# The Mamba block between two attention stacks: chunks of 512 tokens, decays and B read from PSUM, one input product on POOL

## What is computed

```
x = x + 0.5 * ffn_stack(layernorm(x))
x = x + mamba(layernorm(x))
x = x + 0.5 * ffn_stack(layernorm(x))

def mamba(x):                                   # D_INNER 256, D_STATE 16, DT_RANK 64
    h = x * rsqrt(mean(x * x) + 1e-5) * norm_w
    u, res = split(h @ in_w, 2)
    u = silu(causal_conv4(u) + conv_b)
    dt, B, C = split(u @ x_proj_w)
    delta = softplus(dt @ dt_w + dt_b)
    dA, dBu = exp(delta * A), delta * u * B     # per channel and state
    s_t = dA_t * s_(t-1) + dBu_t ;  y_t = sum over states of s_t * C_t
    return ((y + u * D) * silu(res)) @ out_w + x
```

## Time and profile before

| | us |
|---|---|
| runs | 3680.3, 3685.1, 3695.39 |
| median | 3685.1 |
| profiled execution | 3695.99 |
| span of its trace | 3694.2 |
| Mamba block in it, 1630.2 to 2066.1 on the trace's clock | 435.9 |
| of that: until the first input product of the loop (1702.6) | 72.4 |
| loop, until the last scan ends (2052.0) | 349.4 |
| tail | 14.1 |

### The profile page before, as it was taken

The page is one execution under the profiler, slowest core; times in us unless marked ns, Lnnn a source line. Parts: engine busy times, 40 slices in busy tenths (PEclk is TensorE's granted clock), DMA queues, the critical chain, the costliest instruction groups (busy, mean ns, idle before and its releaser), DMA issues. The chain is left out here.

```text
span 3694.2 us, 121091 instructions
## 1 busy us (share of the span) xinstructions
PE 3288.0 (89%) x51496; PEld 2550.1 (69%) x51496; DVE 2961.8 (80%) x3156; ACT 2500.4 (68%) x3070; POOL 2416.0 (65%) x1172
## 2 busy tenths in 40 slices
PE   6999999999999999876766599999999999999997
PEld 4777777777777877742222378777777777777775
DVE  6888888888888878739999778788888878878884
ACT  4777777777777776656333377777777777777764
POOL 5676777677676776602555577767667767767662
PEclk8999999999999999987667799999999999999999
DMA  3333333333233332210000133333323333323222
GB/s 97 86 75 82 70 77 83 69 78 87 65 82 82 74 73 66 66 28 0 0 0 0 46 90 70 72 81 81 84 64 80 85 70 75 87 67 80 65 63 55
DMA packets 160307, 245.34 MB, mean 66 GB/s; under 512 B 50784, under 2 KB 52640, under 8 KB 159648
## 3 DMA queue, kind: packets, MB, share of 16 engines
q1 hardware_dynamic: 159776, 237.59, 26.7%
HBM read 35.01 MB, written 1.05 MB: 10 GB/s over the span
## 5 line engine op out<-in xcount | busy, mean ns | idle before, releaser
L1252 POOL TENSOR_TENSOR ARENA<-ARENA,RN 128x1024 f32<-128x1024 f32 x192 | 365.3, 1902 | 554.3 <-ACT RN L674 554.3
L231 PE MATMUL PS<-C,ARENA 128*128 128x128 f32 x4608 | 620.4, 278 | 120.4 <-ACT ARENA L684 94.7
L231 PEld LDWEIGHTS PS<-C,ARENA 128*128 128x128 f32 x4608 | 514.9, 142 | 206.1 <-issue 171.7
L1244 POOL TENSOR_TENSOR ARENA<-ARENA 128x1024 f32<-128x1024 f32 x192 | 468.2, 2439 | 271.0 <-DVE ARENA L978 270.2
L187 PE MATMUL PS<-WL,XH 128*128 128x512 f32 x1152 | 494.2, 429 | 42.8 <-DVE ARENA L963 18.4
L737 ACT ACTIVATE ARENA<-PS 64x1024 f32<-64x1024 f32 x384 | 390.4, 1017 | 112.5 <-PE PS L231 109.3
L1238 POOL TENSOR_TENSOR ARENA<-ARENA 128x1024 f32<-128x1024 f32 x192 | 457.5, 2383 | 8.2 <-DVE ARENA L963 8.1
L189 PE MATMUL PS<-WH,XH 128*128 128x512 f32 x1152 | 458.6, 398 | 0.0
L188 PE MATMUL PS<-WH,XL 128*128 128x512 f32 x1152 | 456.8, 397 | 0.0
L353 PE MATMUL PS<-ARENA 128*64 128x64 f32 x12288 | 403.3, 224 | 58.9 <-DVE ARENA L1016 35.0
L353 PEld LDWEIGHTS PS<-ARENA 128*64 128x64 f32 x12288 | 378.4, 139 | 93.5 <-issue 92.4
(11 more groups left out here) (136 smaller groups left out, 6689.2 us busy)
## 6 DMA issues: line engine op xcount, KB each, us to landing
ARENA<-ARENA SPq DMA_DIRECT2D x3072, 64.0 KB
ARENA<-in_wqkv SPq DMA_DIRECT2D x36, 512.0 KB, 5.1
ARENA<-in_wo SPq DMA_DIRECT2D x12, 512.0 KB, 3.8
ARENA<-in_w SPq DMA_DIRECT2D x12, 341.0 KB, 3.4
ARENA<-in_w SPq DMA_DIRECT2D x12, 192.0 KB, 5.4
X<-in_xT SPq DMA_DIRECT2D x4, 256.0 KB, 5.0
out<-X SPq DMA_DIRECT2D x1, 1024.0 KB, 3.9
QKS<-in_qks SPq DMA_DIRECT2D x1, 768.0 KB, 8.4
```

What stands on the lines that cost most here:

```text
L231: last = nc.tensor.transpose(PS[:, slot, 128 * j:128 * j + 128], src[:, 128 * j:128 * j + 128], ident)
L1244: nc.gpsimd.tensor_tensor(KN[n % 2], KN[n % 2], T2, ALU.add).then_inc(k_add, 1)
```

## The change

Only the Mamba block and the DMA waits behind it are touched.

- **Loop.** Steps are now k = (chunk of 512 tokens, state), 4 x 16, each with both channel halves. The tiles that hold both halves are laid out [chunk, half, token]. ACT writes the decays to PSUM (banks 4 and 5, one buffer for each half); the scans, one for each half and 512 tokens long, read them there. The spread of B and C is one fp32r matmul each, into a pair of banks. For half 0 the input product stays on DVE and reads B in PSUM (`drive` in `vector_mamba`); for half 1 it is on POOL and reads the SBUF copy BC (`drive` in `pool_mamba`). POOL's product with C (`read_out`) is one instruction for both halves, 2 x 512 tokens. The carried states are copied by ACT (`keep_state`) and used in three chunk changes instead of one. Sums are accumulated for each chunk, so `sum_up` and the gate product (`gate_out`) come four times with 512 tokens and both halves.
- **Prologue.** One centring matmul gives x minus its mean in PSUM; one variance serves both norms (`MRH` for the merged one, `MRS` for the first). The input projection is no longer copied: convolution and gate read PSUM. dt_b enters as a 65th row of the matmul. Softplus works on 1024 elements at a time.
- **Tiles.** All Mamba tiles in ARENA now start at a multiple of 4 words. No operand of the loop is in TAB.
- **SP.** The loads of the second stack wait for `m_g`, `m_xs`, `m_hb` and `m_dt` in place of the end of the loop.

The core of the diff:

```diff
@@ tensor_mamba
-            def spread(i):
+            def spread(k):
+                h, n, pair = k // 16, k % 16, 2 * (k % 2)
+                if k >= 2:
+                    pe.wait_ge(m_bev, k - 1)
...
                 for j in range(2):
-                    s = slice(1024 * h + 512 * j, 1024 * h + 512 * j + 512)
-                    last = nc.tensor.matmul(PS[:, slot, 512 * j:512 * j + 512], one, HR[64:128, s])
+                    one = SEL[64:128, n + 16 * j:n + 16 * j + 1].broadcast_to([64, 128])
+                    last = nc.tensor.matmul(PSB[:, pair + j, :], one, HR[64:128, chunks[h]], start=True, stop=True)
...
+            def accumulate(k):
+                pe.wait_ge(m_pr, k + 1)
...
+                for b in range(2):
+                    last = nc.tensor.matmul(PSB[:, 6 + b, :], ident, PR[k % 2][:, b, :], start=n == 0, stop=n == 15,
...
@@ scalar_mamba
+            for p in range(2):
+                act.wait_ge(m_var, 2 * p + 2)
+                act.activation(MRH[:, pairs[p]], var[p], ACT.Ln, bias=eps2, scale=1.0 + 1e-5).then_inc(m_lnh, 1)
+                act.activation(MRS[:, pairs[p]], var[p], ACT.Ln, bias=eps).then_inc(m_lnr, 1)
...
+            def evacuate(k):
+                act.wait_ge(m_db[0], k + 1)
+                if k >= 3:
+                    act.wait_ge(m_pr, k - 2)
+                act.activation(BC[k % 3], PSF[:, 1024 * (k % 2):1024 * (k % 2) + 1024], ACT.Copy).then_inc(m_bev, 1)
...
+            def decay(k, b):
+                if k:
+                    act.wait_ge(m_sc[b], k)
+                act.activation(PSB[:, 4 + b, :], DL[:, h, b, :], ACT.Exp,
+                               scale=NA[:, 16 * b + n:16 * b + n + 1]).then_inc(m_da[b], 1)
...
@@ vector_mamba
+            for c in range(4):
+                for k in range(3):
+                    for b in (1, 0):
...
+                        nc.vector.scalar_tensor_tensor(
+                            UC[:, c, b, e:512], PSF[:, t0 + e:t0 + 512], MP[:, M_CW + 4 * b + k:M_CW + 4 * b + k + 1],
+                            UC[:, c, b, e:512], ALU.mult, ALU.add).then_inc(m_cv, 1)
...
-                    nc.vector.tensor_tensor(DB[m % 4], DU[b][:, s], BB[k % 2], ALU.mult).then_inc(m_db, 1)
+            def drive(k):
+                dve.wait_ge(m_bc, k + 1)
...
+                nc.vector.tensor_tensor(DB0[k % 2], DU[:, k // 16, 0, :], PSB[:, 2 * (k % 2), :], ALU.mult).then_inc(m_db[0], 1)
...
-                    nc.vector.tensor_tensor_scan(ST[m % 3], DA[m % 2], DB[m % 4], CS[:, col:col + 1] if h else 0.0,
+                nc.vector.tensor_tensor_scan(ST[k % 3][:, b, :], PSB[:, 4 + b, :], (DB0, DB1)[b][k % 2],
+                                             CS[:, 2 * n + b:2 * n + b + 1] if h else 0.0,
...
@@ pool_mamba
-                    nc.gpsimd.tensor_tensor(DB[m % 4], ST[m % 3], CB[k % 2], ALU.mult).then_inc(m_pr, 1)
+            def drive(k):
+                pool.wait_ge(m_bev, k + 1)
...
+                nc.gpsimd.tensor_tensor(DB1[k % 2], DU[:, k // 16, 1, :], BC[k % 3][:, 0:512], ALU.mult).then_inc(m_db[1], 1)
+
+            def read_out(k):
+                pool.wait_ge(m_sc[0], k + 1)
+                pool.wait_ge(m_sc[1], k + 1)
+                if k >= 2:
+                    pool.wait_ge(m_y, k - 1)
+                c = BC[k % 3][:, 512:1024].unsqueeze(1).broadcast_to([128, 2, 512])
+                nc.gpsimd.tensor_tensor(PR[k % 2], ST[k % 3], c, ALU.mult).then_inc(m_pr, 1)
```

More of the change, by code:

```diff
@@ L518, in tensor_mamba @@
+            pe.wait_ge(mw_in, 64)
             for c in range(4):
[L519 to L530, removed]
+                pe.wait_ge(m_hb, c + 1)
+                pe.wait_ge(m_lnr, c // 2 + 1)
+                nc.tensor.matmul(PSB[:, 4 + c, :], INW[:, 128:256], hb[:, chunks[c]], start=True, stop=True).then_inc(m_u, 1)
@@ L558, in accumulate, with delta @@
[L558 to L567, removed]
+            def delta(c):
+                pe.wait_ge(m_xd, c + 1)
+                pe.wait_ge(m_re, min(2 * c + 2, 4))
+                if c >= 2:
+                    pe.wait_ge(m_xl, 2 * c - 2)
+                    pe.wait_ge(m_xd, 2 * c - 2)
+                for b in range(2):
+                    last = nc.tensor.matmul(PSB[:, 2 * c + b, :], DTW[:, 128 * b:128 * b + 128], HB[0:65, chunks[c]],
+                                            start=True, stop=True)
+                last.then_inc(m_dt, 1)
@@ L901, in spread @@
[L901 to L920 removed]
+                act.activation(HR[64:96, chunks[c]], PSB[64:96, 4 + c, :], ACT.Copy)
@@ new lines, in sum_up @@
+            def sum_up(h):
+                dve.wait_ge(m_y, 16 * h + 16)
+                for b in range(2):
+                    nc.vector.scalar_tensor_tensor(Y[:, h, b, :], UC[:, h, b, :], MP[:, M_D + b:M_D + b + 1],
+                                                   PSB[:, 6 + b, :], ALU.mult, ALU.add).then_inc(m_yd, 1)
+            drive(0)
+            for k in range(64):
+                if k < 63:
+                    drive(k + 1)
+                scan(k, 0)
+                if k % 16 == 1 and k > 1:
+                    sum_up(k // 16 - 1)
+                scan(k, 1)
@@ L1198, in vector_mamba @@
+            sum_up(3)
+            dve.wait_ge(m_xs, 4)
+            for c in range(4):
                 dve.wait_ge(m_out, c + 1)
-                if c == 0:
-                    dve.wait_ge(m_xs, 1)
-                nc.vector.tensor_tensor(X[:, s], X[:, s], PS[:, c, 0:512], ALU.add).then_inc(m_done, 1)
+                nc.vector.tensor_tensor(X[:, chunks[c]], X[:, chunks[c]], PSB[:, c, :], ALU.add).then_inc(m_done, 1)
         def pool_stack(pool, r):
```

392 lines of the change are left out of this document (186 added, 206 removed).

## The result

| | before | after |
|---|---|---|
| median of four runs, us | 3687.3 (3680.3 to 3695.4) | 3564.1 (3554.9 to 3573.2) |
| ratio, 95% interval | | 0.9665 (0.9632 to 0.9698) |
| profiled execution, us | 3696.0 | 3554.9 |
| its span | 3694.2 | 3553.0 |
| the Mamba block in it, start and end | 1630.3 and 2066.1: 435.8 | 1624.0 and 1931.9: 307.9 |

The change makes the kernel 3.35% faster, 123 us between the medians. The forecast was 3567. Between the spans of the profiled executions the difference is 141.2 us: 127.9 of it is the block, and 13.3 lies in the two stacks, whose code is the same. So the stacks differ by 10 us and more from one execution to the next, and from here on I compare blocks, not whole spans.

What follows compares the result with a forecast made beforehand. Bound: DVE's input product, POOL's product with C and the scan run one after another. Prologue, POOL's loop, chunk changes, tail and clock sum to a 317.4 us block against 435.9, so 3567 us; range 3528 to 3605.

Steps and rivals of the forecast that it cites:

- The rival that the scan excludes POOL even with one input in PSUM: Loop: POOL's products and both scans run one after another, 5.9 us a step, 147 us more, 3714; chance 0.05.
- start to first product on DVE: Prologue: from its start to DVE's first input product, 61.7 us.
- start to P1 of k = 1: Prologue: from its start to POOL's input product of step k = 1, 66.0 us.
- P1: Loop: POOL's input product of 512 elements, taken at 1.27 us.
- clock, at two places of the prologue: Prologue: PE at the low clock level at two places where it follows idling, adding 2 us.
- a step: Loop: POOL is the slowest engine and its two products take 3.62 us per k.
- from P1 of k = 1 to the end of the last P2, chunk changes' 3 included: Loop: 63 x 1.27 + 64 x 2.35 + 3 x 2.35, with 3 us for chunk changes; 240.5 us.
- P2: Loop: POOL's product with C for both halves, taken at 2.35 us.
- tail: After the last P2: sum, `sum_up`, gate, projection, addition and latencies, 8.9 us.
- the rival of 3617: Loop: PE stays at 1.2 GHz, 4.4 us a step, 50 us more; chance 0.10.
- The slow scan: Loop: scans from PSUM or semaphores slow DVE, 1.6 us a scan, 18 us more, 3585; chance 0.08.
- The short kind: Loop: POOL's products take their shorter duration, 3.07 us a step, 36 us less, 3531; chance 0.15.

Runs made afterwards that it cites:

- e2: The changed kernel with both halves' decays written to SBUF in place of PSUM; ratio 0.9990 against the kernel before, block 429.2 us.
- e5: The changed kernel with only half 1's decays in SBUF, half 0's still in PSUM; ratio 0.9825 against the kernel before, block 365.1 us.
- e1: The changed kernel with the B and C tiles moved by 2 words; ratio 0.9579 against the kernel before, block 280.7 us.
- e6: The kernel before with its state tiles moved by 1 word and its decay tiles by 4; ratio 0.9994, block 430.9 us.
- e4: The changed kernel with only POOL's output tiles moved by 2 words; ratio 0.9664 against the kernel before, block 308.5 us.
- e9: The changed kernel with the B and C tiles moved by 1 word; ratio 0.9583 against the kernel before, block 280.4 us.

## Why the prediction was right

**The bound of the kernel before** was read rightly: not DVE's 98%, but two engines in turn. e2 is the proof, since it brings the turns back without anything else, and the loop is then as slow as the old one (351.5 us against 343.9). The old kernel's own trace held the test already: the pair at 1883.54 and 1884.72 in the earlier trace rows is the same contrast as e5's two rows of scans. The rival that the scan excludes POOL even with one input in PSUM (3714) would have given a kernel like e2, at 3696. The Trainium skill (Perfetto Trace Analysis, section Optimizing Scalar/DVE Operations) warns that moving work between these engines may not help because of their shared port; e2 and e5 bear that out where both inputs are in SBUF, and the kernel after shows that it doesn't hold for a scan that reads one from PSUM.

**The sum, term by term**, in us (the rows in brackets are parts of others):

| term | predicted | measured |
|---|---|---|
| (start to first product on DVE) | 61.7 | 60.4 |
| start to P1 of k = 1 | 66.0 | 64.5 |
| clock, at two places of the prologue | 2 | in the row above |
| (a step) | 3.62 | 3.54 |
| from P1 of k = 1 to the end of the last P2, chunk changes' 3 included | 240.5 | 233.8 |
| tail | 8.9 | 9.6 |
| block | 317.4 | 307.9 |

The prologue, from 1624.0 (first and last of its marks, and three between; L881 the second Exp of the last pair, L1164 the convolution from PSUM, L893 the last SiLU, L912 the last of softplus):

```profile
1637.02 2.01 ACT L881 ACTIVATE ARENA<-ARENA 128x1024 f32<-128x1024 f32 x2
...
1641.79 15.87 DVE L1164 SCALAR_TENSOR_TENSOR ARENA<-PS,MP,ARENA 128x509 f32<-128x509 f32 x24
...
1661.58 1.07 ACT L893 ACTIVATE ARENA<-PS 128x512 f32<-128x512 f32 x2
...
1680.37 1.06 ACT L912 ACTIVATE ARENA<-ARENA 128x1024 f32<-128x1024 f32 x1
...
1684.41 1.29 DVE L1184 TENSOR_TENSOR ARENA<-ARENA,PS 128x512 f32<-128x512 f32 x2
```

Against the marks of the working: 15.0 (15.7), 33.7 (35.4), 38.7 (40.5), 57.4 (59.2), 60.4 (61.7). The convolution started at 17.8 where the working has 19.1; its 24 steps took 15.87, 0.66 each in place of 0.69, another 0.4; and DVE's last two instructions before the first product gave some of it back. The chain ran as laid out: DVE to 1657.7, then ACT.

**The loop** is where 6.7 of the 9.5 us went, and 5.0 of them are the step (63 x 0.08); the prologue and its 2 us for the clock are 3.5, and the tail cost 0.7 more than predicted. The terms mis-sized are the two products of POOL, added up from their durations. P2 and P1 were taken at 2.35 and 1.27, and their least values are 2354 and 1272; yet the step is 3.54, not 3.62, and the medians (2446 + 1363) would even make 3.81. The records overlap: at 1714.40 P2 is shown to start, while P1, shown from 1713.17, is shown to end at 1714.52. A sum of records, least or median, is not a pitch; the starts are. From P1 of k = 1 to the end of the last P2, 63 x 3.54 + 2.4 + 3 x 2.38 = 232.6 of the measured 233.8. So of the 3 us for chunk changes 1.2 were used, most of them in one place: behind the second change PE idles 3.20 us, two sums take 3.78 each at a granted clock of 0.50 (1817 to 1826), and POOL waits 0.57 at 1826.22. At the first change DVE waits for PE as foreseen, and POOL only runs the gate product:

```profile
1747.30 1.41 DVE L1203 SCALAR_TENSOR_TENSOR ARENA<-ARENA,MP,PS 128x512 f32<-128x512 f32 x2 [1.02 <-PE PS L589]
...
1752.34 2.38 POOL L1335 TENSOR_TENSOR ARENA<-ARENA 128x1024 f32<-128x1024 f32 x1
```

**The clock** rose as expected (0.96 in the stretch above) but for the chunk changes, and with it went the rival of 3617. Before, 0.69, with PE idle 3.70 at a time; in e2, where PE is kept waiting again, 0.67:

```profile
1740.00:1780.00 40.00, 29.30 (x45) 9.95 (x44) 40.00 (x22) 17.12 (x29) 31.50 (x15) 0.67 0.00 1
```

**The slow scan** (3585) fell: 1.28 at the most, and DVE's records fill 38.6 of 44 us.

**The short kind** (3531) was rightly ruled out for this kernel, but by a rule that was half wrong. All tiles a multiple of 4 words apart are long, and that was all the prediction needed; its "otherwise short" fails for a distance of 3. Its price was too high: 36 us by steps of 3.07 against 3.62, where e1 gained 27 by 3.01 against 3.54 less the waits behind the chunk changes. The 4497 ns that the prediction takes from the Trainium skill (GPSIMD Engine Reference, section Elementwise — side-by-side cycle accounting) is given there for an add; the 2.25 us worked out from it lies between the two kinds measured here, 2.00 and 2.35, and is neither.

**The tail** took 9.6 us for 8.9. The gate waits 3.56 after the last P2, for sum and `sum_up`, as in the working. Most of the 0.7 lies behind the gate: from its end (1928.17) to the start of the last addition it is 3.03 us, where the working had 2.0 for the projection and a share of 0.5 for latencies:

```profile
1925.82 2.35 POOL L1335 TENSOR_TENSOR ARENA<-ARENA 128x1024 f32<-128x1024 f32 x1 [3.56 <-DVE ARENA L1203]
...
1931.20 0.69 DVE L1218 TENSOR_TENSOR X<-X,PS 128x512 f32<-128x512 f32 x1 [1.03 <-PE PS L604]
```

**The last step, to the median**, was nearer than its parts. The block gained 9.4 us more than predicted, and the median after is only 3 below the forecast. The median before less the block's 128 would be 3557 to 3559; the runs gave 3564, within their own 18 us of spread. So the 3 us are partly luck. For the block after, 9.5 is the fair size of the error. For the gain it is as much, or some 5 less if the kernel before owed 5 us of its block to the clock, as the comparison with e6 suggests.

## What to carry to other kernels

Where DVE and POOL both look busy, compare an instruction's least duration with its median before counting work: if the median is far above, look who runs beside it, and give DVE one of its two inputs from PSUM before shifting work from one engine to the other (here 121 us against less than 5, which can't be told from nothing). Where POOL is then the bound, look at the distance of its two inputs modulo 4 words. Work out a pitch, the distance between the starts of two steps, from starts and not from durations.

## What the runs showed that I had not expected

- **POOL's two-input fp32 product has two durations, set by the distance of its inputs.** 2.00 or 2.35 us for 1024 elements a partition, 1.09 or 1.27 for 512: short for d = 1 and 2, long for d = 0 and 3. That it isn't symmetric (1 and 3 differ) shows that the order of the two inputs counts. The output's address made no difference (e4, one shift, with d = 0). Why, no run shows; that exchanging the inputs turns 3 into 1 follows from the rule, and wasn't tried.
- **A product or scan that has stood waiting for the other engine is 0.1 to 0.2 us shorter when its turn comes**: P1 1.07 behind a scan against 1.27 free, the scan 1.08 against 1.2 to 1.28 (e5). I conclude that its start is already behind it; this is an inference from the rows.
- **POOL's records grow along a chunk without the pitch growing**: P2 from 2.35 to 2.55, overlapping the next by 0.04 to 0.25, and back after the gate product. In e1 and e9 the growth is small (2.00 to 2.04). Its cause stays open; it costs nothing that the starts show.
